# A two-layer graph and mixture network on one core: W2 pieces, diagonals, squares and the output of its end moved

## The reference

```python
# 8 groups x 16 heads = 128 heads of 128; s = 625 tokens; L = 100 pooled keys
qk = einsum('bsghd,blgd->bghsl', q, kc) / 128 ** 0.5
z = einsum('bghsl,blgd->bsghd', softmax(qk), vc).reshape(b, s, 16384)
zn = l2norm(z) * wz_g1                 # one norm for a token, over all heads
h1 = silu(zn @ wz_w1 + wz_b1)          # 16384 -> 1024
h1n = l2norm(h1) * wz_g2
out = silu(h1n @ wz_w2 + wz_b2)        # 1024 -> 512
return x + out
```

## Time and profile before

| what | us |
|---|---|
| median of 3 runs | 2242.36 (2237.57 to 2242.71) |
| the profiled execution's own time | 2241.42 |
| its span | 2239.7 |
| PE busy | 2126.6 (95%) |
| DVE busy | 1514.3 (68%) |
| ACT busy | 1121.6 (50%) |
| POOL busy | 869.9 (39%) |
| all queued DMA | 197.43 MB, 88 GB/s in the mean |

### The profile page before, as it was taken

One profiled execution on the slowest core, in us unless ns is written; L12 is line 12 of the kernel. 1 busy time (PEld: TensorE's weight loads), 2 busy tenths in 40 slices (PEclk: granted clock), 3 DMA queues, 4 the chain that ended last, 5 costly groups with the idle time before them and its releaser, 6 DMA issues.

```text
span 2239.7 us, 36121 instructions
## 1 busy us (share of the span) xinstructions
PE 2126.6 (95%) x13358; PEld 1983.3 (89%) x13358; DVE 1514.3 (68%) x3178; ACT 1121.6 (50%) x3001; POOL 869.9 (39%) x701
## 2 busy tenths in 40 slices
PE   8876799999879999999999999999999999999986
PEld 7765566669769999999999999999999999999985
DVE  8745788864336777766777766777767777767746
ACT  4543566642435555545555545555545555545533
POOL 0000000000234555554555544555545555545552
PEclk9876999999979999999999999999999999999988
DMA  6000688870111112121112121112121112211100
GB/s 207 2 18 4 212 278 278 284 259 10 42 65 61 61 61 99 65 78 61 61 61 99 66 77 61 61 61 102 68 73 61 61 62 101 72 68 61 57 24 23
DMA packets 85613, 197.43 MB, mean 88 GB/s; under 512 B 5862, under 2 KB 10246, under 8 KB 85436
## 3 DMA queue, kind: packets, MB, share of 16 engines
q1 hardware_dynamic: 85437, 195.12, 25.5%
HBM read 193.75 MB, written 1.35 MB: 87 GB/s over the span
## 4 chain that ended last, share of the span: by engine, by line
PE 87%; ACT 5%; DVE 4%; issue 2%; POOL 1%; DMA 1%; SPq 0%; DVEq 0%; POOLq 0%; ACTq 0%
PE PS L54 78%; PE PS L53 5%; PE PS L57 3%; ACT HW L88 1%; ACT GT L88 1%; ACT HS L88 0%; DMA X<-in_x 0%; ACT EE L88 0%; POOL SM L60 0%; DVE OHs L68 0%; DVE SM L107 0%; DMA RAW<-in_L_ffn_wz_w 0%; POOL WS L60 0%; DVE M L75 0%; DVE JU L66 0%
## 5 line engine op out<-in xcount | busy, mean ns | idle before, releaser
L54 PE MATMUL PS<-ZH,WS 128*128 128x314 f32 x4096 | 952.5, 313 | 9.0 <-POOL WS L60 6.7
L54 PEld LDWEIGHTS PS<-ZH,WS 128*128 128x128 f32 x4096 | 696.3, 190 | 9.8 <-POOL WS L60 7.2
L54 PE MATMUL PS<-ZL,WS 128*128 128x314 f32 x2048 | 628.3, 307 | 0.0
L60 DVE TENSOR_TENSOR ACC<-ACC,PS 128x314 f32<-128x314 f32 x1008 | 476.0, 476 | 207.1 <-PE PS L54 197.5
L54 PEld LDWEIGHTS PS<-ZL,WS 128*128 128x128 f32 x2048 | 390.2, 191 | 0.0
L60 POOL TENSOR_TENSOR WS<-RAW,WS 128x512 fp32r<-128x512 f32 x256 | 327.7, 1301 | 106.4 <-ACT WS L88 106.3
L60 POOL TENSOR_TENSOR ML<-MF,MH 128x400 fp32r<-128x400 f32 x128 | 134.0, 1047 | 414.9 <-ACT MH L88 414.7
L60 POOL TENSOR_TENSOR ZS<-ZS,ZQ 128x628 f32<-128x628 f32 x128 | 198.2, 1549 | 237.2 <-ACT ZQ L88 237.2
L88 ACT ACTIVATE ZH<-PS,g1T 128x628 fp32r<-128x628 f32 x128 | 100.4, 785 | 322.0 <-PE PS L54 322.0
L88 ACT ACTIVATE EE<-EE,SM 125x100 f32<-125x100 f32 x640 | 233.4, 375 | 13.8 <-DVE SM L68 11.0
L88 ACT ACTIVATE MF<-PS 128x400 f32<-128x400 f32 x128 | 64.6, 505 | 320.6 <-PE PS L53 320.6
(11 more groups left out here) (332 smaller groups left out, 3751.0 us busy)
## 6 DMA issues: line engine op xcount, KB each, us to landing
RAW<-in_L_ffn_wz_w SPq DMA_DIRECT2D x66, 1024.0 KB, 5.4
RAW<-in_L_ffn_w SPq DMA_DIRECT2D x64, 1024.0 KB, 7.3
RAW<-in_L_ffn_Wq_w SPq DMA_DIRECT2D x32, 1024.0 KB, 5.4
CB<-c_rows SPq DMA_DIRECT2D x32, 195.3 KB
RAW<-in_L_gnn_W SPq DMA_DIRECT2D x4, 1024.0 KB, 8.8
RAW<-in_L_ffn_Wkv_w SPq DMA_DIRECT2D x4, 1024.0 KB, 5.2
RAW<-in_L_ffn_Wk_T SPq DMA_DIRECT2D x2, 1024.0 KB, 5.8
WB<-w_rows SPq DMA_DIRECT2D x6, 305.2 KB
```

What stands on the lines that cost most here:

```text
L54: return self.q.matmul(o, l, r, start=start, stop=stop)
L60: return Nothing() if self.q is None else self.q.tensor_tensor(out=o, in0=a, in1=b, op=op)
```

## The change

1. `sp_ffn1`: each of the five stores of 125 rows becomes two, of 120 and of 5 rows; the final wait counts ten.
2. W2's pieces, on ACT and on POOL: instead of four in iteration 129 and four in iteration 130, ahead of other work, two in each of the iterations 130 to 133, behind W1's pieces.
3. The five diagonals go from POOL (iteration 133) to DVE (iteration 134, behind four tile additions). DVE's clamp, inverse and scale go there as well. POOL's power stays in iteration 133, now behind the pieces. DVE's copy of the norm sums goes to the end of iteration 133, and PE's norm sums behind all eight tiles of it; PE's rows product goes ahead of the last two tiles of iteration 134.
4. A Silu on one column is added on ACT in iteration 133.
5. The squares of the hidden tiles go from POOL to ACT (`Square`), behind the copy to H1H.
6. DVE's order: only tile 0 is scaled in iteration 134; in iteration 135 `hidden(m + 1)` is ahead of `hidden_lo(m - 1)` and `squares(m - 2)`. ACT does all eight tiles behind the loop.

```diff
 (sp_ffn1)
-                q.dma(out[P * t:P * t + P, :], X[:, t, :]).then_inc(s_out, 16)
-            q.wait_ge(s_out, 16 * T5)
+                for lo, hi in ((0, 120), (120, 125)):
+                    q.dma(out[P * t + lo:P * t + hi, :], X[lo:hi, t, :]).then_inc(s_out, 16)
+            q.wait_ge(s_out, 32 * T5)
 (g_ffn1)
-                if NH + 1 <= i < NH + 3:
-                    for k in range(4):
-                        piece(2, i - NH - 1, k)
...
-                if i == LAST - 2:
-                    q.wait_ge(*rz_v.of("cp"))
-                    g_power(q, rz, rz, hp[0:P, 0:5], rz_g, "norm")
-                    q.wait_ge(*rz_v.of("rz"))
-                    q.wait_ge(*lg_v.of(NH // 4 - 1, "add", 4))
-                    for t in range(T5):
-                        j = q.ts(DG[:, t, :], ident[0:P, 0:P], rz[:, t:t + 1], None, ALU.mult)
-                    j.then_inc(*rz_g.up("diag"))
                 r, part = (i - 6) // 2, (i - 6) % 2
                 if 0 <= r < NH // 2:
                     piece(1, r, 2 * part)
                     piece(1, r, 2 * part + 1)
...
+                if NH + 2 <= i < NH + 6:
+                    for k in range(2):
+                        piece(2, (i - NH - 2) // 2, 2 * (i % 2) + k)
+                if i == LAST - 2:
+                    q.wait_ge(*rz_v.of("cp"))
+                    g_power(q, rz, rz, hp[0:P, 0:5], rz_g, "norm")
 (a_ffn1)
                 q.act(H1H[:, m, :], ACC[:, m, :], ACT.Copy, scale=miT[:, 12 + m:13 + m]).then_inc(*h1_a.up(m, "hi"))
+                if m >= 2:
+                    q.wait_ge(*h1_sum.of(m - 2))
+                q.act(SQT[:, m % 2, :], ACC[:, m, :], ACT.Square).then_inc(*h1_sq.up(m))
...
+                if NH + 2 <= i < NH + 6:
+                    for k in range(2):
+                        piece(2, (i - NH - 2) // 2, 2 * (i % 2) + k)
+                if i == LAST - 2:
+                    q.act(wsm[:, 6:7], ones[0:L, 0:1], ACT.Silu).then_inc(*f_a.up("silu 2"))
...
-            for m in range(6, 8):
+            for m in range(8):
                 hidden(m)
 (v_ffn1)
                     for m in range(4):
                         for a in todo[2 * m:2 * m + 2]:
                             wz(*a)
-                        hidden_lo(m)
-                        squares(m)
-                        hidden(m + 2)
+                        if m < 3:
+                            hidden(m + 1)
+                        if m >= 1:
+                            hidden_lo(m - 1)
+                        if m >= 2:
+                            squares(m - 2)
...
-                if i == LAST - 2:
-                    q.wait_ge(*rz_mm.of("ss"))
-                    q.cp(rz, PS[0:P, 1, 0:5]).then_inc(*rz_v.up("cp"))
+                if i == LAST - 1:
                     q.wait_ge(*rz_g.of("norm"))
...
+                    q.wait_ge(*rz_v.of("rz"))
+                    for t in range(T5):
+                        j = q.ts(DG[:, t, :], ident[0:P, 0:P], rz[:, t:t + 1], None, ALU.mult)
+                    j.then_inc(*rz_v.up("diag"))
...
+                if i == LAST - 2:
+                    q.wait_ge(*rz_mm.of("ss"))
+                    q.cp(rz, PS[0:P, 1, 0:5]).then_inc(*rz_v.up("cp"))
                 if i == LAST - 1:
-                    for m in range(2):
-                        hidden(m)
-            for m in range(4, 8):
+                    hidden(0)
+            for m in range(3, 8):
+                if m < 7:
+                    hidden(m + 1)
                 hidden_lo(m)
-                squares(m)
-                if m + 2 < 8:
-                    hidden(m + 2)
+                squares(m - 1)
+            squares(7)
 (pe_ffn1)
+                for a in todo[4:6]:
+                    wz(*a)
+                if i == LAST - 1:
+                    q.wait_ge(*rz_v.of("diag"))
...
+                    free[0] = free[1] = rz_a.of()
+                for a in todo[6:]:
+                    wz(*a)
                 if i == LAST - 2:
                     q.wait_ge(*z_sum.of(NH - 1))
...
-                for a in todo[4:]:
-                    wz(*a)
-                if i == LAST - 1:
-                    q.wait_ge(*rz_g.of("diag"))
...
-                    free[0] = free[1] = rz_a.of()
```

More of the change, by code:

```diff
@@ L1944, in z_ @@
                 q.tt(ZS[:, :], ZS[:, :], ZQ[:, :], ALU.add).then_inc(*z_sum.up(h))
[L1946 to L1951, removed]
             for t in range(T5):
@@ L2145, in a_ffn1 @@
                 if i == LAST:
-                    for m in range(4):
-                        hidden(m + 2)
                     continue
@@ L2561, in pe_ffn1 @@
                     attT(i - 5)
+                for a in todo[4:6]:
+                    wz(*a)
+                if i == LAST - 1:
+                    q.wait_ge(*rz_v.of("diag"))
+                    q.wait_ge(*free[0])
+                    q.wait_ge(*free[1])
+                    for t in range(T5):
+                        o = PS[:, 0, P * t:P * t + P] if t < 4 else PS[:, 1, 0:P]
+                        j = q.mm(o, ones[0:P, :], DG[:, t, :], True, True)
+                    j.then_inc(*rz_mm.up("rows"))
+                    free[0] = free[1] = rz_a.of()
+                for a in todo[6:]:
+                    wz(*a)
                 if i == LAST - 2:
```

3 lines of the change are left out of this document (removed).

## The result

| | us |
|---|---|
| kernel before, median of 4 runs | 2240.63 (2237.57 to 2242.71) |
| changed kernel, median of 4 runs | 2213.38 (2210.37 to 2215.61) |
| ratio, 95% interval | 0.9872 (0.986 to 0.9885) |
| changed, profiled execution: own time, span | 2215.61, 2213.6 |

The changed kernel is faster by 1.3%; 2215 was forecast, in a range of 2209 to 2223.

The account below looks back on a forecast made before the run. PE was taken as full at clock 1.00 until 2126 us, with gains only in its last iterations and the output. -6.5 - 6.9 + 0.9 - 8.3 - 6.4 = -27.2 from 2241.42 gave 2214.2, 2215 as median; range 2209 to 2223.

Parts of the forecast that it names:

- (a): Iteration 130: PE waits for POOL's W1 pieces queued behind W2's; W2 in pairs behind W1 was to give -6.5 us.
- (b): Iteration 134: PE waits for W1's last pieces behind POOL's five diagonals; -6.9 us, and +0.9 for PE awaiting DVE's diagonals.
- the eight tiles of iteration 135: PE's eight tiles of the W1 product at full clock: 6.94 us instead of 10.22, so -3.3.
- last product to the norm sum: PE's thirty groups of three matmuls: 21.0 us instead of 26.75, so -5.75; +0.7 for DVE freeing PSUM bank 4.
- (c): Iteration 135 and last product: DVE late beside POOL's square; squares on ACT and scaling sooner were to give -8.3 us.
- output: Final stores in 120 and 5 rows, fifteen DMA engines instead of five: 3.5 us after DVE's last addition, not 9.9; -6.4.
- The narrow margin at W1's pair: Iteration 129: POOL has W1's pair ready at 2127.4, PE wants it at 2127.6; margin 0.2 us.
- a cover of 3.4: ZS of head 127 ready at 2156.4, PE reads it at 2159.8; 3.4 us cover delays from W2's pairs on POOL.
- Bank 4: Iteration 135: DVE's addition frees PSUM bank 4 at 9.0 us, PE wants it at 8.3; +0.7 (0 to 2).
- tables change to and fro: Rival: ACT's Square and Silu share no table, so sixteen loads of 1.28 us; time 2230, chance 0.03.
- part of the holes stays: Rival: one PE hole over 2 us remains, costing itself and about 2.7 of half clock; time 2220, chance 0.14.
- the slower rival: PE's clock falls to 0.50 in iteration 130 and stays down: up to 73 us more, time up to 2288, chance 0.02.

## Why the prediction was right, point by point

The steps from the traces, in us:

| step | forecast | trace of the changed kernel | undone alone |
|---|---|---|---|
| (a) W2 in pairs, iterations 130 to 132 | -6.5 | -6.63 | 6.81 |
| (b) and the eight tiles of iteration 135 | -6.9 + 0.9 - 3.3 | -9.38 | power 6.63, engine of the diagonals 1.82 |
| last product to the norm sum | -5.75 + 0.7 | -5.22 | |
| (c) in all, squares and order | -8.3 | -8.4 | both 7.61 |
| output | -6.4 | -6.90 | 6.85 |
| sum | -27.2 | -28.1 | |

The row of (c) overlaps the two above it: its -8.4 are the eight tiles of iteration 135 (7.0 us for them, from ten tiles in 8.79 us between 2169.71 and 2178.50, instead of 10.22) and the -5.22. Every part came out a little larger than forecast, none the other way. That the medians fall by 27.25 us, the forecast's figure, is in part luck: the stretch gained 28.14, the profiled execution gave 2.0 of it back in front of the loop, and the medians carry the same scatter.

**(a)** The mechanism and the size are shown, in both directions. The narrow margin at W1's pair held, 0.25 us for the forecast's 0.2. On ZS I had a cover of 3.4; it is 3.2. The pieces on POOL are somewhat slower than costed (a pair 3.0 at 2137.74, not 2.5).

**(b)** That POOL's order made the hole is shown. The reason was incomplete: I named the five diagonals, and for the kernel before its trace bears that out (an estimate, above). But in the changed kernel, where the norm sums come 3.5 us later, the power alone, because it waits, brings the same hole (6.63 us). So the power, too, has to stand behind the pieces there; the prediction names its new place and gives it no price. The diagonals on DVE are 1.06 us for five, under my 1.45, and the wait is 0.45, not 0.9.

**(c)** The size is right and the reason was half of it. The sentence that DVE is late in (c) beside POOL's square names one cause; the other, DVE's old order, it doesn't price. In the old order the square is worth 3.4 us of the 7.61, in the new one 0.87; the order is worth 4.17 even with the squares on ACT. The sum went by what PE would gain once DVE kept up, and so it didn't need the split: had the change moved the squares alone, the same sum would have been some 4 to 5 us too high (an estimate). ACT's tile was costed at 0.82 for the square, which takes 0.71. Bank 4 costs 0.28, not 0.7. The two edits undone don't bring all 8.4 back; the first hole is 1.47 there and 2.29 in the kernel before. There the first Silu stands behind a table load (1.28 us) and the rows product two tiles later; which of the two makes the difference wasn't tested.

**Output** The mechanism is shown by 125, 120 and 124 rows; that it is exactly fifteen engines is not. The term was undersized by half a us, the tail being 3.0 and not 3.5, and two of its parts were wrong in opposite directions. Behind the last issue data moves until 2212.7, 1.4 us and not 0.8, since the stores run at 183 GB/s in the mean and not at the 309 that fifteen times 20.6 would give. From there to the span's end are 0.9 us and not 1.9; in the kernel before, too, the last data moves at 2238.9, and not at the forecast's 2237.8.

**Rivals.** That tables change to and fro is refuted by the single load. That part of the holes stays didn't happen. Its price had an error: it added 2.7 of half clock to a wait of 2 us, and a wait of 2.38 us before the rows product, instead of 0.45, cost 1.82 in all, at clock 1.00. In the changed kernel the clock is 1.00 as long as PE has work in the stretch, so the slower rival's condition didn't come. Where it did come, with W2's pieces in fours, the clock was back at 1.00 from 2137 on.

## What to carry to other kernels

Where a matmul engine is full for most of a kernel, look for the waits in its last iterations, and ask of each what stands ahead of the awaited instruction in its queue: a short operation that itself waits can cost as much as a long one. Behind a hole of a few us there may be a stretch at half clock, so an order can be worth more than the waits that it removes: here 1.3 to 1.9 times where the clock fell (7.61 us for 5.9 of waits, 6.81 for 3.7), and no more than the waits where it didn't (1.82 for 1.9). Check that the rows of a last store have a large divisor up to 16, and undo the parts of a change one by one and together, since two causes of one wait need not add. When a part is put back alone, look whether what it waits for still stands where it stood.

## What the runs showed of the hardware that I had not expected

The length of a hole doesn't by itself tell whether half clock follows. Holes of 1.28, 1.47 and 2.38 us had clock 1.00 behind them. One of 2.29 us in the kernel before had clock 1.00 for another us and then 0.51:

```profile
2190.00 0.41 PE L54 MATMUL PS<-ZH,WS 128*128 128x314 f32 x1 [2.29 <-DVE ACC L60]
```

```profile
2190.00:2191.00 1.00, 1.00 (x7) 1.00 (x8) 1.00 (x2) 0.97 (x2) 0.52 (x1) 1.00 0.00 0
2191.00:2194.00 3.00, 3.00 (x11) 2.70 (x11) 3.00 (x5) 0.62 (x2) 1.21 (x1) 0.51 0.00 0
```

Holes of 2.63 us and more had 0.50 at once. And stores through four engines moved 102 GB/s, as much as through five (103 and 104), so the rate of one engine isn't fixed: 25.5 GB/s against 20.6. What holds it there with five engines stays open.
